# Gated unit of a graph network in row order: rows stationary, the weights of three gates moving

## The reference

```python
deg = sum(adj, axis=1) + 1e-6;  d = rsqrt(deg)
x1  = layernorm(x + (d[:, None] * (adj + I) * d[None, :]) @ (x @ W0))
msg = relu((adj @ x1) @ W_msg.T + b_msg)
gi, gh = msg @ W_ih.T + b_ih, x1 @ W_hh.T + b_hh      # three gates of 128 each
r = sigmoid(i_r + h_r);  z = sigmoid(i_z + h_z);  n = tanh(i_n + r * h_n)
out = layernorm(x1 + (1 - z) * n + z * x1)
```

## Time and profile before

| what | value |
|---|---|
| median of 3 runs | 1808.65 (1807.96 to 1808.85) |
| profiled execution: time | 1809.21 |
| profiled execution: span, first to last instruction | 1807.4 |
| TensorE busy, mean granted clock | 1664.8 (92%), 0.974 |
| VectorE busy | 1449.1 (80%) |
| ScalarE busy | 726.8 (40%) |
| GpSimd busy | 138.9 (8%) |
| moved by DMA | 551.12 MB |

### The profile page before, as it was taken

How to read it: one execution, slowest core, us unless ns; L and a number is a source line. 1 busy time by engine, 2 the same in 40 slices (tenths; PEclk the granted TensorE clock), 3 DMA queues, 4 the chain that set the end, 5 groups by cost and what they waited for, 6 DMA issues and landing times.

```text
span 1807.4 us, 17022 instructions
## 1 busy us (share of the span) xinstructions
PE 1664.8 (92%) x6444; PEld 1169.4 (65%) x6444; DVE 1449.1 (80%) x1380; ACT 726.8 (40%) x713; POOL 138.9 (8%) x111
## 2 busy tenths in 40 slices
PE   0088799997999999999999999999999999999997
PEld 0043354442444456888888888888788888888886
DVE  7888899999999966776666655665788988889897
ACT  0000011111111123445444444444576767666774
POOL 0000000000000011000000000000002121212121
PEclk8589999999999999999999999999999999999998
DMA  9999999999999982666666556656999999999993
GB/s 393 421 378 421 421 421 421 422 421 422 420 421 421 421 321 93 204 196 198 199 203 194 193 193 200 201 187 194 338 325 302 319 316 317 314 309 319 310 317 112
DMA packets 181393, 551.12 MB, mean 305 GB/s; under 512 B 13440, under 2 KB 14464, under 8 KB 148544
## 3 DMA queue, kind: packets, MB, share of 16 engines
q1 hardware_dynamic: 177824, 541.38, 81.3%
q0 software_dynamic: 2480, 8.13, 1.4%
q10 hardware_dynamic: 1008, 0.53, 0.1%
HBM read 545.79 MB, written 4.19 MB: 304 GB/s over the span
## 4 chain that ended last, share of the span: by engine, by line
PE 83%; DMA 13%; DVE 3%; POOL 0%; ACT 0%; SPq 0%; issue 0%; DVEq 0%; POOLq 0%; ACTq 0%
PE bank L460 21%; PE bank L511 18%; PE bank L513 18%; PE bank L512 18%; DMA kept<-adj_blocks 6%; DMA ring<-adj_blocks 4%; DMA pool<-adj_blocks 3%; PE bank L584 1%; PE bank L583 1%; PE bank L582 1%; DVE colsum L909 1%; PE bank L443 1%; PE bank L434 1%; PE bank L482 1%; PE bank L578 1%; PE bank L570 0%
## 5 line engine op out<-in xcount | busy, mean ns | idle before, releaser
L931 DVE TENSOR_TENSOR lo<-ring,hi 128x2048 fp32r<-128x2048 f32 x206 | 470.4, 2289 | 248.9 <-ACT f L772 205.5
L761 ACT ACTIVATE hi<-ring 128x2048 fp32r<-128x2048 f32 x206 | 395.3, 1919 | 368.5 <-DMA ring<-adj_blocks 245.3
L511 PE MATMUL bank<-hi,x1s 128*128 128x512 f32 x1016 | 406.3, 400 | 3.3 <-DVE lo L931 2.4
L513 PE MATMUL bank<-hi,x1s 128*128 128x512 f32 x1016 | 396.9, 391 | 0.0
L512 PE MATMUL bank<-lo,x1s 128*128 128x512 f32 x816 | 318.3, 390 | 0.0
L460 PE MATMUL bank<-kept,feat 128*128 128x512 f32 x656 | 290.9, 595 | 20.6 <-DMA kept<-adj_blocks 20.6
L460 PEld LDWEIGHTS bank<-kept,feat 128*128 128x128 f32 x656 | 122.9, 190 | 179.9 <-issue 154.3
L909 DVE TENSOR_TENSOR colsum<-colsum,kept 128x2048 f32<-128x2048 f32 x93 | 213.2, 2292 | 20.5 <-DMA kept<-adj_blocks 18.9
L511 PEld LDWEIGHTS bank<-hi,x1s 128*128 128x128 f32 x1016 | 191.2, 188 | 46.0 <-issue 3.6
L739 ACT ACTIVATE part<-bank 128x512 f32<-128x512 f32 x72 | 39.1, 595 | 444.5 <-PE bank L460 444.5
L513 PEld LDWEIGHTS bank<-hi,x1s 128*128 128x128 f32 x1016 | 191.0, 188 | 40.8
(11 more groups left out here) (152 smaller groups left out, 1723.4 us busy)
## 6 DMA issues: line engine op xcount, KB each, us to landing
ring<-adj_blocks SPq DMA_DIRECT2D x412, 512.0 KB, 5.2
kept<-adj_blocks SPq DMA_DIRECT2D x147, 1024.0 KB, 14.9
ring<-adj_blocks SPq DMA_DIRECT2D x56, 1024.0 KB, 15.0
pool<-adj_blocks SPq DMA_DIRECT2D x53, 1024.0 KB, 14.8
more<-adj_blocks SPq DMA_DIRECT2D x100, 512.0 KB, 5.6
xt<-x_t SPq DMA_DIRECT2D x8, 512.0 KB, 14.0
xin<-x POOLq DMA_DIRECT2D x16, 256.0 KB, 3.3
out<-y POOLq DMA_DIRECT2D x15, 256.0 KB, 3.8
```

The lines of the kernel that those rows point to most:

```text
L511: pe.matmul(acc[:, :], fh, ah, start=start and c == 0, stop=False, skip_group_check=True)
L513: mm = pe.matmul(acc[:, :], fl, ah, start=False, stop=stop and c == KC - 1, skip_group_check=True)
L761: ins = act.activation(hi[:, n % NHI], raw(slot_of2[n]), ACT.Copy)
L931: ins = dve.tensor_tensor(flat(low(n)), flat(raw(slot_of2[n])), flat(hi[:, n % NHI]).bitcast(f32), ALU.subtract)
```

## The change

The gates are computed in row order. A bank of PSUM now holds, for 128 rows, four groups of 128 columns: i_n, r, z (negated), h_n. The stationary operand is 128 rows of x1 or of the message, the moving one is the weights of three gates side by side (384 columns); `h_step` and `gates_step` have twelve products each instead of nine. The biases are spread over a tile `bias4` once, by a product of ones with diagonal matrices early in the kernel, and ScalarE copies that tile into the four banks for every row (`seed_gates`) before the products add to them. x1 in row order is summed by GpSimd from its two parts into `xin` (`xsum`, one row ahead), TensorE transposes it four times for the transposed layout, and the new state stays in row order, so `rows_step` and `last_rows` are gone. The two sigmoids become one of twice the size. `out_stats` and `out_step` stand at 12 and 14. At the start only the first weight matrix and three bias vectors are loaded, VectorE waits for the biases before it sums, and the other matrices are loaded after the first stage. PSUM banks are dealt out anew.

The core of the diff:

```diff
             def x1t_step(i):
                 g = gru_no[i]
+                pe.wait_ge(xsum_ready, g + 1)
...
+                for c in range(KC):
+                    mm = pe.transpose(p_x[:, c * 128:(c + 1) * 128], xin[:, g % 2, c, :], ident[:, :])
+                mm.then_inc(x1t_done, 1)
...
+            def gates(c, cols, xh, xl, wh, wl, stop):
+
+                of = slice(c * 128, (c + 1) * 128)
+                pe.matmul(quad[:, c, cols], xh[:, of], wh[:, :], start=False, stop=False, skip_group_check=True)
+                pe.matmul(quad[:, c, cols], xl[:, of], wh[:, :], start=False, stop=False, skip_group_check=True)
+                return pe.matmul(quad[:, c, cols], xh[:, of], wl[:, :], start=False, stop=stop, skip_group_check=True)
...
-                i = gru_row(n, 11)
-                if i is not None:
-                    rows_step(i)
...
+            act.dma_start(w0_s[:, :], w0).then_inc(w0_in, 16)
+            for dst, src in biases:
+                act.dma_start(dst, src).then_inc(biases_in, 16)
...
+            def seed_gates(i):
+                g = gru_no[i]
+                if g == 0:
+                    act.wait_ge(y_ready, NT)
+                    act.wait_ge(bias_ready, 1)
+                else:
+                    act.wait_ge(npre_ready, g)
+                for c in range(KC):
+                    ins = act.activation(quad[:, c, :], bias4[:, :, :].rearrange("p q d -> p (q d)"), ACT.Copy)
+                ins.then_inc(gates_seeded, 1)
...
+            for dst, src in weights:
+                act.dma_start(dst, src).then_inc(weights_in, 16)
             for n in range(2):
                 hi_tile(n)
...
                 i = gru_row(n, 5)
                 if i is not None:
+                    seed_gates(i)
                     x1t_step(i)
...
+            dve.wait_ge(biases_in, 48)
             dve.wait_ge(consts, 2)
...
+                i = gru_row(n, 12)
+                if i is not None:
+                    out_stats(i)
                 i = gru_row(n, 14)
                 if i is not None:
-                    out_stats(i)
-                if n == NN:
-                    last_sum()
-                i = gru_row(n, 16)
-                if i is not None:
                     out_step(i)
+            last_sum()
...
+            def xsum(g):
+
+                i = rows3[g]
+                if g < 2:
+                    pool.wait_ge(x1_whole, NT)
+                else:
+                    pool.wait_ge(x1t_done, g - 1)
+                    pool.wait_ge(new_ready, g - 1)
+                pool.tensor_tensor(xin[:, g % 2], x1s[:, i * KC:(i + 1) * KC, 0, :].bitcast(f32),
+                                   x1s[:, i * KC:(i + 1) * KC, 1, :].bitcast(f32), ALU.add).then_inc(xsum_ready, 1)
+
+            xsum(0)
+            xsum(1)
             for g, i in enumerate(rows3[:-1]):
+                if 1 <= g < NT - 1:
+                    xsum(g + 1)
                 deviation(NT + g)
```

More of the change, by code:

```diff
@@ L309, in gnn_resnorm_kernel @@
         brz = sb("brz", [128, 2])
[L310 to L311 removed]
+        weights = [(wmsg_s[:, :], wmsg_t), (wih_s[:, :], wih_t), (whh_s[:, :], whh_t)]
+        biases = [(bih_s[:, :], b_ih), (bhh_s[:, :], b_hh), (bmsg_s[:, :], b_msg)]
         NW = len(weights)
[L314 removed]
+        quad = ctx.enter_context(nc.psum_tensor("quad", [128, KC, W], f32))
+        bank = [quad[:, c, :] for c in range(KC)]
+        bank += [ctx.enter_context(nc.psum_tensor(f"bank{i}", [128, W], f32)) for i in range(KC, 8)]
         p_supp, p_deg = (bank[4], bank[5]), bank[7]
[L316 to L319 removed]
+        acc0, acc1, tr = (bank[0], bank[1]), (bank[6], bank[7]), (bank[4], bank[5])
+        p_x, p_msg = bank[4], bank[5]
+        g_in, g_rz, g_hn = quad[:, :, 0:D], quad[:, :, D:3 * D], quad[:, :, 3 * D:4 * D]
+        g_hidden, g_input = slice(D, 4 * D), slice(0, 3 * D)
+        last_msg_bank = (bank[5], bank[4])
         def slot(s):
@@ L628, in last_tile @@
                     mm.then_inc(halves_done, 1)
[L630 to L634, removed]
             def last_h(h):
-                xh, xl = x1th[:, half(h)], x1tl[:, half(h)]
                 pe.wait_ge(x1t_split, G + 1)
[L639 to L642, removed]
+                pe.wait_ge(gates_seeded, G + 1)
+                for c in (2 * h, 2 * h + 1):
+                    gates(c, g_hidden, x1th, x1tl, whhh_s, whhl_s, False)
             def last_msg(h):
@@ L869, in _ @@
                     n_step(i)
+                if n == NN - 3:
+                    seed_gates(last_row)
             x1t_step(last_row)
@@ L1090, in last_npre @@
             def last_npre(h):
-                dve.wait_ge(rz_ready, G + 1 + 2 * h)
+                own = slice(2 * h, 2 * h + 2)
+                dve.wait_ge(rz_ready, G + 1 + h)
                 dve.wait_ge(diff_done, 2 * G)
-                dve.scalar_tensor_tensor(gn[:, half(h)], p_n2[h][:, half(1)], bhh_s[:, 2:3], gr[:, half(h)], ALU.add, ALU.mult)\
-                   .then_inc(nmul_done, 1)
+                dve.tensor_tensor(gn[:, own, :], g_hn[:, own, :], rz[:, own, 0, :], ALU.mult).then_inc(nmul_done, 1)
@@ L1101, in last_npre @@
+                dve.wait_ge(out_ready, G)
+                dve.scalar_tensor_tensor(newt[:, own, :], rz[:, own, 1, :], -2.0, xin[:, G % 2, own, :], ALU.add, ALU.mult)\
                    .then_inc(last_u, 1)
             def last_newt(h):
+                own = slice(2 * h, 2 * h + 2)
                 dve.wait_ge(n_ready, G + 1 + h)
-                dve.tensor_tensor(gn[:, half(h)], gn[:, half(h)], gz[:, half(h)], ALU.mult).then_inc(diff_done, 1)
+                dve.tensor_tensor(gn[:, own, :], gn[:, own, :], rz[:, own, 1, :], ALU.mult).then_inc(diff_done, 1)
@@ L1106, in last_newt @@
                 dve.wait_ge(last_u, h + 1)
                 dve.wait_ge(diff_done, 2 * G + 1 + h)
-                dve.tensor_tensor(newt[:, half(h)], gn[:, half(h)], newt[:, half(h)], ALU.subtract).then_inc(last_new, 1)
+                dve.tensor_tensor(newt[:, own, :], gn[:, own, :], newt[:, own, :], ALU.subtract).then_inc(new_ready, 1)
             def last_norm(h):
                 at = NT + G
-                dve.wait_ge(rows_done, G + 1 + h)
-                for c in range(2):
-                    ins = dve.bn_stats(stats[:, at % 2, 2 * h + c, :], p_msg2[h][:, c * D:(c + 1) * D])
+                dve.wait_ge(new_ready, G + 1 + h)
@@ L1140, in _ @@
             x1_lo(whole[0])
-            for n in range(2, NN + TAIL):
-                if n < NN:
-                    split_lo(n)
+            for n in range(2, NN):
+                split_lo(n)
                 i = normed_row(n, 2)
```

214 lines of the change are left out of this document (98 added, 116 removed).

## The result

The changed kernel takes 1816.54 (median of 5 runs, 1816.01 to 1818.35), the kernel before 1808.65 in its 5 runs (1807.63 to 1809.25). The ratio is 1.0046, 95% interval 1.0031 to 1.0061: slower, by more than the 0.2% that a measurement of this kernel can tell from no change. The profiled execution has a span of 1814.2 against 1807.4.

The account below looks back on a forecast made before the run. TensorE was taken to bound the gated rows, with VectorE's splits barely ahead of it. Rows +9.8, additions +0.4, start -1.1, end +0.1, first row's transposes -0.4 sum to +8.8: 1817.5, range 1812 to 1824.

Parts of the forecast that it names:

- The mechanism and its price: Gated rows: statistics put ahead of a tight VectorE split make TensorE wait; +0.70 a row, +9.8 over 14 gaps.
- the gates' 0.05: Gate products on TensorE: 24 of 384 columns replacing 18 of 512 cost +0.05 a row, bounds 0 and 0.15.
- The wait of 1.3: Once per gated row, TensorE waits 1.3 for the VectorE split that the moved statistics delay.
- both leads, 0.67 and 0.72: Gated row's two tightest tiles: splits ready 0.67 and 0.72 before TensorE starts them, behind `new_step` and `agg_step` respectively.
- the first rival: Gated rows: the statistics find room in VectorE's order, so TensorE's saving of 13.0 comes off; 1796, chance 0.09.
- its lower bound: GpSimd's 128x512 addition in each row: 1.2 as lower bound, costing 0; upper bound 2.3, costing 0.4 a row.
- The third rival: Gated rows: GpSimd's addition binds too, at 2.3 or more, putting off VectorE splits; 1823 to 1830, chance 0.10.
- The start: First loads: 0.46 MB of weights leaving this stretch gives -1.1, bounds -1.1 and +5; VectorE's sums start near 15.3.
- the bound for late biases: First stage: biases arriving as late as the seventh load make it end 5 later; 1823, chance 0.06.
- The passage to the third stage: Before regular rows: first two GpSimd additions meet splits, +0.4; the first row's own transposes give -0.4.
- The end: End chain: last transposes leave, 0.70; one larger sigmoid +0.2; statistics delay the last two splits 0.7 each; sum +0.1.
- The clock as a rival: Gated rows: the granted clock falls at each new TensorE wait, 14 x 1.7 = 24; 1841, chance 0.05.

## Why the prediction was right, point by point

**The mechanism and its price** were as predicted. From the start of e+9 to that of e+13 it gave 1537.01 - 1524.17 = 12.84; the trace has 1538.31 - 1525.52 = 12.79. The row was to be 0.70 longer and is 0.71 longer: 12.79 is 0.50 more than the 12.29 of before (0.55 predicted), and 0.21 come behind it (0.15 predicted), of which the restart is 0.10. The rest is spread over products that follow each other at 0.23 to 0.24 after a restart, and was not taken apart. That the sum agrees to the hundredth is luck in part: the gates' 0.05 was not there, the loss up to e+13 was 0.05 smaller, and this rest, 0.11, was not foreseen. That the statistics do this is shown from three sides: out of the way (13 or 14) the wait is gone and 15 us with it, doubled they lengthen the row by their own length where the clock stays up, and doubled work on TensorE, ScalarE or GpSimd does not lengthen the row.

**The wait of 1.3** is split in two: 1.11 ahead of e+13 and 0.19 ahead of e+12 (0.51 and 0.80 in the two rows of the new block, the same sum). The prediction had both leads, 0.67 and 0.72, and compared only the second with the change. It missed that TensorE's own saving of 0.84 is more than the first lead: e+12 becomes late whatever is done with the statistics. In the kernel after this changes no number, because e+13 is later still. But it is what the first rival's price got wrong: "It decides above a lead of 1.2" is one condition where there are two, and a third in two rows of 14, the bank that `agg_step` has to empty. With the statistics moved the time is 1801.9, not 1796; with a piece of `new_step` moved too it is 1793.9.

**TensorE.** Transposes 0.44 instead of 0.84, none for the result: as predicted. The gates cost nothing: 12 products take 2.10 (1513.08 to 1515.18), 0.175 each, and 9 of before took 2.09 (1511.78 to 1513.87). The 0.05 of the row was not there.

**ScalarE** costs nothing, and at twice the seeds still nothing in the rows. **GpSimd** works for 1.2 to 1.3, its lower bound, but its instruction lies in the trace for 7.25 and ends at 1550.93, 1.15 after VectorE's split of 1547.49 to 1549.78. The third rival had it put off splits. It is the other way: three VectorE instructions begin and end while it waits, and it gets its turn when VectorE is idle. The Trainium skill (SBUF — State Buffer, Who interferes with whom) says that one of the two holds the other off for a whole instruction, whichever began first. The trace agrees that it is one or the other: in the run with the addition twice the splits from 1287 on took 3.31 with an addition each. It does not agree on the order: in the rows the addition is there from 1543.69, and three VectorE instructions that began later went ahead of it. In the rows it is GpSimd alone that is held.

**The start** gave -1.4 by 90 us and -2.0 by 705, predicted -1.1. The first sum came at 14.62, predicted near 15.3, and the bound for late biases was named well: behind the weights they cost 5.7. But the 0.46 MB of weights explain only the 1.2 at 90 us. The kernel with all weights at the start is 0.1 ahead of the kernel before there (90.65 and 90.79) and 1.7 ahead at the end of the stage (705.88 and 707.55), 1.3 of it by the second panel's sums (225.18 and 226.44). So most of what the start had gained by 705 does not come from the term that the prediction named, and no run here shows where it comes from.

**The passage to the third stage** was predicted at 0 (+0.4 for the additions, -0.4 for transposes) and gave -1.0. TensorE's wait there is 1.02 instead of 2.4 (at 1281.38 and at 1284.09), and the granted clock stays at 1.00 where it had been 0.72. Against that stand the first two additions, which cost more than the 0.4: the tiles of 1290.71 and 1294.01, whose splits they hold up, start 0.42 and 0.45 late, and the next product of each 0.11 late, 1.1 together. The change can hardly claim the shorter wait. The same wait is 2.0 in the two kernels with moved statistics (clock 0.88 and 0.79 in 1284 to 1290), 2.5 in the one with the weights at the start (0.79) and 1.1 in the one with `new_step` cut (1.00), though the written order of that passage is the same in all of them as in the kernel after. Each was profiled once. This wait, 1.0 to 2.5 over all these kernels, differs by up to 1.4 for reasons that no experiment here touched; a term below that can't be read from two profiled spans.

**The end** gave -0.2, predicted +0.1; the working of that term was not tested. The chain's end shows the step that had to go gone: between `newt` and its statistics there is no TensorE link any more.

```profile
1809.03 0.44 DVE newt L1115
...
1809.49 0.50 DVE stats L1121 x2
```

**The clock as a rival** was put at 0.05 and did not come about, but the doubled statistics show it close by: of twelve waits of 1.82 to 1.87 nine were followed by it. Why these and not the other three stays open.

## What to carry to other kernels

In a stream whose engines work in a written order, a saving on the busiest engine is worth nothing until each of the tight hand-overs has room for it: list the leads of all of them over one period, take the saving off each, and only then ask what the moved work adds. Here 0.84 was saved and two leads were 0.67 and 0.72, and a third, the bank of a new block, was nothing in two rows of 14. 1.2 us of small work one position too early cost 15 us, and moving three steps (the statistics, the output, the last operation of `new_step`) behind the tight splits turned +0.5% into -0.8%. To find out whether an engine sets the period, double its work at the suspected place: the period answers at once, and an answer of nothing is as clear as the other. Look at the clock in such a run too: the longer wait can bring its own loss, as the doubled statistics did.

## What the runs showed of the hardware

- GpSimd's addition of 128x512 with two inputs takes 1.30 alone. Issued in a row during a split, with two more splits and a smaller operation behind that without a pause, it lasted 7.25 and held none of them up (2.24 in the kernels with the statistics at 14); issued at the start of the third stage, two to four of them took turns with splits that also followed each other without a pause, 3.2 to 3.3 an addition and 3.31 a split. What decides between the two was not found. Where it got its turn while VectorE was idle, the split behind it took up to 2.99 instead of 2.29 (that of 1287.66 in the kernel after).
- The same wait of TensorE, 1.86 and 1.87, was followed by the lower clock level in one row and not in another; over a kernel, nine of twelve waits of 1.82 to 1.87 were. Waits of 0.92 to 0.96 in 12 rows of the kernel after never were. Ahead of the third stage the waits of 2.0 to 2.5 in four kernels each were, and those of 1.0 to 1.8 in the seven others were not.
- After a wait the first product holds up the next: 0.31 to 0.34 instead of 0.23, in every restart shown here at the full clock. A gap of 0.2 for which the profile names no releaser costs 0.3 in this way.
- Products of 512, 384 and 256 columns follow each other after 0.23, 0.175 and 0.12: in these the width sets the time, and nothing is lost by the cut into three gates.
